# One attention slot on TensorE, in another order

## The chip, the core and the metric

The kernel runs on one core of a Trainium2 chip. The metric is the device time of the whole program in microseconds (us). TensorE (PE) does the matrix products, ScalarE (ACT) the exponentials and most copies out of PSUM, VectorE (DVE) the reductions and the arithmetic on products, GpSimd (POOL) some elementwise work and the indirect DMAs, SyncE (SP) issues the other DMAs. Each engine takes its instructions in the order in which the program gives them; between engines only semaphores order the work.

## The reference

```python
h = _layernorm(x, axis=-1) * (1 + ca) + sa
x = x + ga * _L0_attn_ref(h, ...)      # x is (8, 512, 128), 16 heads of width 8
h = _layernorm(x, axis=-1) * (1 + cb) + sb
x = x + gb * _L0_ffn_ref(h, ...)       # a shared expert, and 2 of 8 routed ones per token

# in _L0_attn_ref, with weights that are binarised (sign times mean magnitude)
att = jnp.einsum('bhtd,bhsd->bhts', q, k) * scale
att = jax.nn.softmax(att, axis=-1)
y = jnp.einsum('bhts,bhsd->bhtd', att, v)
return _binlinear(y, Wp, bp)
```

The attention is dense: for each of the 8 batches and 16 heads there is a 512 x 512 matrix of scores.

## The kernel before, in words

The attention takes most of the time. It runs over the 8 batches (0 to 7), and each batch over 16 **slots** (`SLOTS`). A slot is one group of four heads (`n // 4`) and one quarter of the 512 keys (`n % 4`, 128 keys). Four streams of work run through the slots, each at another distance:

- **scores** (L1446, four in a slot, hh = 0 to 3): a 128 x 512 product of keys and queries of one head, into the score banks `st0` and `st1` in turn. Since there are two banks, each waits on `exp_done` until the exponential of the score two before it is done. Queries and keys are stored as three bf16 parts each, and a row of the stack holds the negated maximum, so that the exponential (L803 on ACT, `pt<-st`) needs no more than a scale.
- **fills** (L1431, two in a slot, each two 128 x 512 products): the scores of a later group, eight slots ahead, for which DVE takes row maxima (`neg_max<-mx`, L1012). The first fill of a slot goes to bank pair `mx0`, the second to `mx1`; each waits on `mx_free` until DVE has reduced the fill before the last. In the first five slots of batch 0 there are three fills. In slots 8 to 15 of batch 7 there are none, and scores 2 and 3 are then written to `mx1`, so that four banks hold scores (`wide`, L345); there a score waits for the exponential of the score four before it.
- the **weighted sum** (L1457, `products`): four 32 x 512 float32 products of one slot's exponentials and values, into `pv`, accumulated over eight slots. It belongs to the slot before and waits for all four exponentials of that slot. The sums that begin an accumulation (those of slots 0 and 8) wait also on `y_evacuated`, the copy of `pv` by ACT (`evacuate_y`, L809).
- **misc work**: one bank, `misc`, for all the small products. `between` (L1524) issues one piece in most slots. In batches 1 to 5 these are: slots 1, 5 and 9 a transpose of maxima (`max_T`, L1364), 2 and 11 a transpose of the weighted sums, 3 a transpose of the normalised sums, 4 the output projection, 7 a transpose of a layer norm, 8 and 14 the projections to queries and keys for the batch two on, 10 a transpose for the second layer norm, 12 the router logits. Slots 0, 6, 13 and 15 have none there. At the end of slot 0 stands the value projection (L1357), at the end of 12 one more transpose of maxima, at the end of 15 the ranks (L1402).

Every order is written by hand. `body` at L1553 gives PE's; `body` at L864 ACT's: four exponentials of slot n, then copies such as `evacuate_y` (after slots 0 and 8), the copy of the value projection (L794, after slot 0) and of the query projection (L788, after slot 8); `body` at L1120 DVE's: the reduction of the first fill, then the work on misc results and layer norms, then the reduction of the second fill. The two buffers `pt` of exponentials alternate by slot.

After the attention come the shared expert (L1590, L1600) and the routed experts (L1646, L1655).

Of the kernel before, what the change touches and what calls it, by code (L numbers as in the profile page):

```python
# [18 lines left out]
SLOTS = G * TT  # L19
# [28 lines left out]
def adaln_block(nc: bass.Bass, x, Wq, bq, Wk, bk, Wv, bv, Wp, bp, sh_gate, sh_up, sh_down,  # L48
                gate_w, up_w, down_w, router_w, routing_bias, c, wmod, out):
    ctx = ExitStack()  # L50
    with ctx:
# [306 lines left out]
        def fill_of(f):  # L358

            b, g = f // (2 * HG * G), f // (2 * HG) % G  # L360
            return Batch(b), g, f // 2 % HG, f % 2
# [958 lines left out]
        def _(pe):  # L1320
# [27 lines left out]
            def project(i, done):  # L1348

                free(done)  # L1350
                pe.matmul(misc[:], wT[:, i, :], hT[:], start=True, stop=True).then_inc(misc_full, 1)  # L1351
# [172 lines left out]
            def between(b, n, first, last):  # L1524
# [25 lines left out]
                if n == 14 and b.const < B - 2:  # L1550
                    project(1, use(b, "k"))

            def body(b, first, last):  # L1553
                for n in range(SLOTS):
                    g, j = n // TT, n % TT
                    fills = fills_at(b, n)
                    if j == 0:
                        pe.wait_ge(m_row_loaded[g % 2], ROW_DMAS * (2 * b.n + g // 2 + 1))
                        if b.const == 0 and g < DIRECT:
                            pe.wait_ge(stack_loaded[0][g], STACK_DMAS)  # L1560
                    scores(b, n, 0)
                    scores(b, n, 1)
                    for f in fills[0]:
                        max_scores(*fill_of(f))
                    between(b, n, first, last)
                    scores(b, n, 2)
                    for f in fills[1][:1]:
                        max_scores(*fill_of(f))
                    scores(b, n, 3)
                    for f in fills[1][1:]:  # L1570
                        max_scores(*fill_of(f))

                    if n > 0:
                        products(b, n - 1)
                    elif not first:
                        products(b.plus(-1), SLOTS - 1)
                    if n == 0 and not last:
                        project_v(use(b, "v"))
                    if n == 12 and not last:
                        max_T(b.plus(1), 0, use(b, "m0"))  # L1580
                    if n == 15 and not first:
                        ranks(b.plus(-1), use(b, "rank"))

            batches(body)
            def shared_up(b, j):

# [128 lines left out]
```

## Time and profile before

| what | us |
|---|---|
| median of 3 runs | 664.68 |
| lowest and highest run | 662.48 to 667.34 |
| the profiled execution, first to last instruction | 683.7 |
| mean granted TensorE clock of it | 0.971 of full speed |

The profiled execution gives no time beside its span. That span is 19.0 us longer than the median of the runs, so the profile is read for its differences and waits, and a difference is carried over to the median as it is. Times in its rows count from the first instruction. A row of the timeline shows a start, a duration, an engine, a line, an operation and a count; rows of like operations are merged. An idle time in brackets is that of the engine before the row, with what ended it. PE durations overlap, since matrix products are pipelined: what a product costs is read from the distance between two starts.

### The profile page before, as it was taken

To read this page: it belongs to the slowest core of one execution; us is meant where nothing else is said; L and a number is where in the kernel's file an instruction comes from. 1 tells how busy PE (TensorE), PEld (TensorE's weight loads), DVE (VectorE), ACT (ScalarE), POOL (GpSimd) and SP (SyncE) were. 2 spreads that over 40 slices of the span, in tenths; PEclk is the share of its full clock that TensorE was granted. 3 is DMA by queue.
4 is the path that set the end of the run, shared out by engine and by line. 5 is a ranking of instruction groups with operands and counts; after the bars stand their busy time and mean duration, and the time that the engine had idled before them with its cause. 6 is when DMAs were issued, how large, how long until landed. Compare 5 with 4: busy or idle time off the path is not lost.

```text
span 683.7 us, 11593 instructions
## 1 busy us (share of the span) xinstructions
PE 624.5 (91%) x3693; PEld 298.9 (44%) x3693; DVE 516.7 (76%) x1104; ACT 411.0 (60%) x846; POOL 264.0 (39%) x309
## 2 busy tenths in 40 slices
PE   4988999999999999999999999999998898888935
PEld 2332333233333333433333333232465888888931
DVE  5659888889988989888898888983368655555617
ACT  2145777777777687777777777778542445444520
POOL 4221022324352461452434233134434366566540
PEclk9669999999999999999999999999999999999987
DMA  3533132222321233223222231115102222222228
GB/s 101 146 56 97 52 101 76 66 82 72 94 86 62 75 97 95 79 78 105 72 70 75 70 98 52 39 40 173 53 0 70 64 74 78 69 78 79 70 68 320
DMA packets 50064, 56.92 MB, mean 83 GB/s; under 512 B 10281, under 2 KB 39243, under 8 KB 50004
## 3 DMA queue, kind: packets, MB, share of 16 engines
q1 hardware_dynamic: 42648, 43.11, 22.4%
q0 software_dynamic: 4320, 8.47, 3.6%
q10 hardware_dynamic: 3036, 4.61, 2.1%
q8 instruction: 30, 0.49, 0.3%
q14 instruction: 30, 0.25, 0.1%
HBM read 38.36 MB, written 17.92 MB: 82 GB/s over the span
## 4 chain that ended last, share of the span: by engine, by line
PE 68%; DVE 13%; ACT 6%; DMA 4%; issue 4%; SPq 2%; POOL 1%; another core or an unknown queue 0%; ACTq 0%; POOLq 0%; DVEq 0%
PE pv L1457 15%; PE st L1446 14%; PE mx L1431 13%; PE st L1646 9%; DVE neg_max L1012 6%; PE mx L1590 3%; ACT pt L803 2%; PE misc L1324 2%; PE misc L1351 2%; PE pv L1655 2%; PE misc L1655 2%; PE st L1600 1%; PE misc L1357 1%; DMA even_qk<-k_parts 1%; DVE ln L969 1%
## 5 line engine op out<-in xcount | busy, mean ns | idle before, releaser
L803 ACT ACTIVATE pt<-st 128x512 f32<-128x512 f32 x496 | 282.2, 598 | 106.0 <-PE st L1446 96.8
L1012 DVE TENSOR_REDUCE neg_max<-mx 128x2 f32<-128x1024 f32 x248 | 294.4, 1215 | 50.5 <-PE mx L1431 47.3
L1457 PE MATMUL pv<-pt,vs 128*32 128x512 f32 x1024 | 136.4, 605 | 0.3 <-ACT pt L803 0.3
L690 POOL DMA_INDIRECT routed<-rec,row_u x64 | 64.4, 1007 | 142.1 <-PE pv L1457 115.2
L750 POOL DMA_INDIRECT results<-qs,home_u x71 | 77.4, 1091 | 60.5 <-ACT qs L932 42.1
L1446 PE MATMUL st<-even_qk 74*128 74x512 bf16 x256 | 88.9, 388 | 4.1 <-DMA even_qk<-m_rows 2.2
L1446 PE MATMUL st<-qs,ks 74*128 74x512 bf16 x240 | 81.5, 383 | 1.8 <-ACT pt L803 1.1
L1431 PE MATMUL mx<-even_qk 72*128 72x512 bf16 x240 | 74.5, 392 | 6.0 <-DVE neg_max L1012 3.4
L1431 PE MATMUL mx<-ks,qs 72*128 72x512 bf16 x256 | 76.5, 380 | 2.8 <-DVE neg_max L1012 2.5
L1258 DVE TENSOR_TENSOR vs<-vs,st 128x256 f32<-128x256 f32 x71 | 29.7, 418 | 42.6 <-ACT vs L927 31.4
L1646 PE MATMUL st<-vs,pt 128*128 128x128 f32 x376 | 52.0, 282 | 10.3 <-DVE vs L1258 7.4
L398 POOL TENSOR_TENSOR qk_r<-qk_f,qk_parts 128x512 f32<-128x512 f32 x15 | 17.4, 1163 | 108.6 <-DVE qk_parts L390 108.4
L927 ACT ACTIVATE vs<-st 128x256 f32<-128x256 f32 x71 | 27.4, 386 | 45.7 <-PE st L1646 35.1
L1446 PEld LDWEIGHTS st<-even_qk 74*128 74x128 bf16 x256 | 20.7, 98 | 73.2 <-ACT pt L803 51.6
L1646 PEld LDWEIGHTS st<-vs,pt 128*128 128x128 f32 x376 | 46.8, 196 | 12.8 <-ACT vs L922 9.1
L1446 PEld LDWEIGHTS st<-qs,ks 74*128 74x128 bf16 x240 | 18.9, 98 | 67.5 <-ACT pt L803 51.6
L1457 PEld LDWEIGHTS pv<-pt,vs 128*32 128x32 f32 x1024 | 20.1, 108 | 52.9 <-issue 38.1
L1431 PEld LDWEIGHTS mx<-even_qk 72*128 72x128 bf16 x240 | 22.3, 100 | 37.9 <-DVE neg_max L1012 11.6
L1431 PEld LDWEIGHTS mx<-ks,qs 72*128 72x128 bf16 x256 | 23.8, 98 | 31.0 <-DVE neg_max L1012 7.8
L1270 DVE COPY pt<-even_qk 128x768 f32 x47 | 27.6, 588 | 6.2 <-issue 3.1
L1590 PE MATMUL mx<-h2T,shared_w 128*128 128x512 f32 x64 | 29.9, 600 | 1.9 <-issue 1.9
L1646 PE MATMUL st<-vs 128*128 128x128 f32 x192 | 25.9, 278 | 3.7 <-DVE vs L1258 2.5
(199 smaller groups left out, 792.7 us busy)
## 6 DMA issues: line engine op xcount, KB each, us to landing
ks<-routed SPq DMA_DIRECT2D x71, 65.0 KB
even_qk<-q_parts SPq DMA_DIRECT2D x48, 96.0 KB
qs<-q_parts SPq DMA_DIRECT2D x48, 96.0 KB
ks<-k_parts SPq DMA_DIRECT2D x48, 96.0 KB
even_qk<-k_parts SPq DMA_DIRECT2D x42, 96.0 KB
q_parts<-qk_parts SPq DMA_DIRECT2D x21, 128.0 KB
k_parts<-qk_parts SPq DMA_DIRECT2D x7, 384.0 KB, 2.3
x_in<-L_attn_x SPq DMA_DIRECT2D x8, 256.0 KB
```

Source lines behind the costliest of these rows:

```text
L690: pool.indirect_dma_start(out=routed_dram, out_offset=bass.IndirectOffsetOnAxis(ap=row_u[:, k, t:t + 1], axis=0), in_=rec[b.par][:, k, t, ...
L750: pool.indirect_dma_start(out=result_dram, out_offset=bass.IndirectOffsetOnAxis(ap=home_u[:, slot:slot + 1], axis=0), in_=y_u[slot], in_of ...
L803: act.activation(pt[n % 2][:, hh, :], score_bank(b, n, hh), ACT.Exp, scale=SCALE).then_inc(exp_done, 1)
L927: act.activation(silu_u[slot % 2], st_bank[slot % 2][:, 0:I], ACT.Silu).then_inc(silu_ready, 1)
L1012: dve.tensor_reduce(neg_max[g % 2][:, hh, 2 * half:2 * half + 2], mx_bank[half][:], AX_X, ALU.max, negate=True).then_inc(mx_free, 1)
L1258: dve.tensor_tensor(act_u[slot % ARING], silu_u[slot % 2], st_bank[slot % 2][:, I:2 * I], ALU.mult).then_inc(act_ready, 1)
L1270: dve.tensor_copy(w_unit[u % WRING], weights.rearrange("p e i -> p (e i)")[:, bass.ds(first, 3 * I)]).then_inc(w_ready, 1)
L1431: last = pe.matmul(mx_bank[half][:, t, :], qs[b.par][0:PROD, h, q0:q0 + P], ks[b.par][0:PROD, h, :], start=True, stop=True)
L1446: pe.matmul(score_bank(b, n, hh), ks[b.par][0:STACK, h, j * P:(j + 1) * P], qs[b.par][0:STACK, h, :], start=True, stop=True).then_inc(st_f ...
L1457: last = pe.matmul(pv_bank[32 * hh:32 * (hh + 1), :], vs[b.par][:, j, HG * g + hh, :], pt[n % 2][:, hh, :], start=(n % Y_SLOTS == 0), stop ...
L1590: last = pe.matmul(mx_bank[j][:, which, :], shared_w[:, IC * which + j, :], h2T[:, T * b:T * (b + 1)], start=True, stop=True)
L1646: last = pe.matmul(st_bank[slot % 2][:, m * P:(m + 1) * P], w_unit[u % WRING][:, m * P:(m + 1) * P], xuT[slot % 2], start=True, stop=True)
```

## The change

In each slot the four scores, two fills, the misc work and the weighted sum of the slot before are put in another order. Nothing is added or taken away, and the instructions of ACT, DVE and SP stay as they are.

```diff
+            def weigh(b, n, first):
+                if n > 0:
+                    products(b, n - 1)
+                elif not first:
+                    products(b.plus(-1), SLOTS - 1)
...
                     scores(b, n, 0)
-                    scores(b, n, 1)
                     for f in fills[0]:
                         max_scores(*fill_of(f))
+                    scores(b, n, 1)
+                    weigh(b, n, first)
+                    scores(b, n, 2)
                     between(b, n, first, last)
-                    scores(b, n, 2)
                     for f in fills[1][:1]:
                         max_scores(*fill_of(f))
                     scores(b, n, 3)
                     for f in fills[1][1:]:
                         max_scores(*fill_of(f))
-
-                    if n > 0:
-                        products(b, n - 1)
-                    elif not first:
-                        products(b.plus(-1), SLOTS - 1)
                     if n == 0 and not last:
                         project_v(use(b, "v"))
```

How the PE instructions then stand, at three places. The first is slot 3 of batch 1, a slot with misc work (the transpose `misc<-ident,y_tok`); `st` are the score banks, `mx` the fills, `pv` the weighted sum. Before:

```order
L1446 MATMUL st0<-qs1,ks1 128x512 [waits exp_done]
L1446 MATMUL st1<-qs1,ks1 128x512 [waits exp_done]
L1431 MATMUL mx0<-ks1,qs1 128x512 [waits mx_free]
L1431 MATMUL mx0<-ks1,qs1 128x512
L1324 MATMUL misc<-ident,y_tok 128x128 [waits misc_free]
L1324 MATMUL misc<-ident,y_tok 128x128 x3
L1446 MATMUL st0<-qs1,ks1 128x512 [waits exp_done]
L1431 MATMUL mx1<-ks1,qs1 128x512 [waits mx_free]
L1431 MATMUL mx1<-ks1,qs1 128x512
L1446 MATMUL st1<-qs1,ks1 128x512 [waits exp_done]
L1457 MATMUL pv<-pt0,vs1 32x512 [waits exp_done]
L1457 MATMUL pv<-pt0,vs1 32x512 x3
```

and after:

```order
L1446 MATMUL st0<-qs1,ks1 128x512 [waits exp_done]
L1431 MATMUL mx0<-ks1,qs1 128x512 [waits mx_free]
L1431 MATMUL mx0<-ks1,qs1 128x512
L1446 MATMUL st1<-qs1,ks1 128x512 [waits exp_done]
L1457 MATMUL pv<-pt0,vs1 32x512 [waits exp_done]
L1457 MATMUL pv<-pt0,vs1 32x512 x3
L1446 MATMUL st0<-qs1,ks1 128x512 [waits exp_done]
L1324 MATMUL misc<-ident,y_tok 128x128 [waits misc_free]
L1324 MATMUL misc<-ident,y_tok 128x128 x3
L1431 MATMUL mx1<-ks1,qs1 128x512 [waits mx_free]
L1431 MATMUL mx1<-ks1,qs1 128x512
L1446 MATMUL st1<-qs1,ks1 128x512 [waits exp_done]
```

The weighted sum stood between score 3 and the next slot's score 0; it now stands between scores 1 and 2, and the misc work stands behind score 2.

The second place is slot 9 of batch 1, where the new accumulation of the weighted sum begins (its first product waits on `y_evacuated`). Before:

```order
L1446 MATMUL st0<-qs1,ks1 128x512 [waits exp_done]
L1446 MATMUL st1<-qs1,ks1 128x512 [waits exp_done]
L1431 MATMUL mx0<-even_qk 128x512 [waits mx_free]
L1431 MATMUL mx0<-even_qk 128x512
L1364 MATMUL misc<-ident,neg_max1 16x128 [waits mx_free,misc_free]
L1446 MATMUL st0<-qs1,ks1 128x512 [waits exp_done]
L1431 MATMUL mx1<-even_qk 128x512 [waits mx_free]
L1431 MATMUL mx1<-even_qk 128x512
L1446 MATMUL st1<-qs1,ks1 128x512 [waits exp_done]
L1457 MATMUL pv<-pt0,vs1 32x512 [waits y_evacuated,exp_done]
```

and after:

```order
L1446 MATMUL st0<-qs1,ks1 128x512 [waits exp_done]
L1431 MATMUL mx0<-even_qk 128x512 [waits mx_free]
L1431 MATMUL mx0<-even_qk 128x512
L1446 MATMUL st1<-qs1,ks1 128x512 [waits exp_done]
L1457 MATMUL pv<-pt0,vs1 32x512 [waits y_evacuated,exp_done]
L1457 MATMUL pv<-pt0,vs1 32x512 x3
L1446 MATMUL st0<-qs1,ks1 128x512 [waits exp_done]
L1364 MATMUL misc<-ident,neg_max1 16x128 [waits mx_free,misc_free]
```

Of the slot's work, two scores, a fill and the transpose of maxima stood ahead of this waiting product and now stand behind it.

The third place is slot 14 of batch 7, without fills and with four score banks (`mx1` holds scores here). Before, to the first score of slot 15:

```order
L1446 MATMUL st0<-qs1,ks1 128x512 [waits exp_done]
L1446 MATMUL st1<-qs1,ks1 128x512 [waits exp_done]
L1446 MATMUL mx1<-qs1,ks1 128x512 [waits exp_done] x2
L1457 MATMUL pv<-pt1,vs1 32x512 [waits exp_done]
L1457 MATMUL pv<-pt1,vs1 32x512 x3
```

and after:

```order
L1446 MATMUL st0<-qs1,ks1 128x512 [waits exp_done]
L1446 MATMUL st1<-qs1,ks1 128x512 [waits exp_done]
L1457 MATMUL pv<-pt1,vs1 32x512 [waits exp_done]
L1457 MATMUL pv<-pt1,vs1 32x512 x3
L1446 MATMUL mx1<-qs1,ks1 128x512 [waits exp_done] x2
```

The weighted sum, which waits for the last exponential of the slot before, now stands ahead of scores 2 and 3.

## Rows read from the trace of the kernel before

**Rows 1.** The page: the chain that ended last, by engine.

```profile
PE 68%; DVE 13%; ACT 6%; DMA 4%; issue 4%; SPq 2%; POOL 1%; another core or an unknown queue 0%; ACTq 0%; POOLq 0%; DVEq 0%
```

**Rows 2.** Windows: one batch: length, busy PE, PEld, DVE, ACT, POOL, clock, DMA.

```profile
109.90:165.60 55.70, 54.52 (x314) 19.39 (x313) 49.50 (x101) 41.34 (x76) 15.88 (x19) 1.00 0.24 72
```

**Rows 3.** Timeline, PE: slot 3 of batch 1, with misc work.

```profile
114.28 0.60 PE L1446 MATMUL st<-qs,ks 74*128 74x512 bf16 x2
114.72 0.60 PE L1431 MATMUL mx<-ks,qs 72*128 72x512 bf16 x2
115.16 0.60 PE L1324 MATMUL misc<-ident,y_tok 128*128 128x128 f32 x4
115.59 0.38 PE L1446 MATMUL st<-qs,ks 74*128 74x512 bf16 x1
...
116.56 1.06 PE L1457 MATMUL pv<-pt,vs 128*32 128x512 f32 x8
117.56 0.39 PE L1446 MATMUL st<-qs,ks 74*128 74x512 bf16 x1
```

**Rows 4.** Timeline, PE: slot 13 of batch 1, without misc work.

```profile
148.90 0.60 PE L1446 MATMUL st<-qs,ks 74*128 74x512 bf16 x2
...
149.97 0.39 PE L1446 MATMUL st<-qs,ks 74*128 74x512 bf16 x1
...
151.94 0.60 PE L1446 MATMUL st<-qs,ks 74*128 74x512 bf16 x2
```

**Rows 5.** Timeline: score 3 of slot 14, batch 1, and its exponential.

```profile
154.51 0.38 PE L1446 MATMUL st<-qs,ks 74*128 74x512 bf16 x1
...
154.93 0.60 ACT L803 ACTIVATE pt<-st 128x512 f32<-128x512 f32 x1 [0.24 <-PE st L1446]
```

**Rows 6.** Timeline: scores 3 of slots 8 and 9, batch 1, and ACT between them.

```profile
134.00 0.38 PE L1446 MATMUL st<-qs,ks 74*128 74x512 bf16 x1
...
135.49 0.60 ACT L809 ACTIVATE y_strips<-pv 128x512 f32<-128x512 f32 x1
135.96 1.10 ACT L803 ACTIVATE pt<-st 128x512 f32<-128x512 f32 x2
...
137.29 0.38 PE L1446 MATMUL st<-qs,ks 74*128 74x512 bf16 x1
```

**Rows 7.** Timeline: DVE in slots 4 to 6 of batch 1, and the fill that waits for it.

```profile
119.77 0.68 DVE L1039 TENSOR_TENSOR x<-misc,x_ep 128x512 f32<-128x512 f32 x1
...
121.55 2.32 DVE L1012 TENSOR_REDUCE neg_max<-mx 128x2 f32<-128x1024 f32 x2
...
125.33 3.47 DVE L1012 TENSOR_REDUCE neg_max<-mx 128x2 f32<-128x1024 f32 x3
126.59 0.60 PE L1431 MATMUL mx<-ks,qs 72*128 72x512 bf16 x2 [0.56 <-DVE neg_max L1012]
```

**Rows 8.** Timeline: weighted sums of slots 4, 7, 12 and 15, batch 1.

```profile
120.29 1.06 PE L1457 MATMUL pv<-pt,vs 128*32 128x512 f32 x8
...
130.62 1.06 PE L1457 MATMUL pv<-pt,vs 128*32 128x512 f32 x8
...
147.79 1.06 PE L1457 MATMUL pv<-pt,vs 128*32 128x512 f32 x8
...
158.08 1.06 PE L1457 MATMUL pv<-pt,vs 128*32 128x512 f32 x8
```

**Rows 9.** Timeline: slots 0 and 1 of batch 2, about the value projection.

```profile
161.25 1.07 PE L1457 MATMUL pv<-pt,vs 128*32 128x512 f32 x8
...
164.66 0.39 PE L1446 MATMUL st<-even_qk 74*128 74x512 bf16 x1 [0.19 <-ACT pt L803]
...
165.63 1.06 PE L1457 MATMUL pv<-pt,vs 128*32 128x512 f32 x8
```

**Rows 10.** Timeline: ACT in slots 14 and 15 of batch 7, without fills.

```profile
478.30 1.09 ACT L803 ACTIVATE pt<-st 128x512 f32<-128x512 f32 x2
...
480.26 1.08 ACT L803 ACTIVATE pt<-st 128x512 f32<-128x512 f32 x2
```

## The prediction, made before the changed kernel ran

> **What bounds the kernel now.** I read the chain of waits first: 68% of it is PE and 13% DVE [rows 1], so the order of PE's own work decides. Then one whole batch by windows: in 55.70 us DVE is busy 49.50 and ACT 41.34 [rows 2]; the window runs from the weighted sum of slot 1 in one batch to that in the next. Busy PE (54.52) says little, because its durations overlap, so I take the distances between starts in the timeline. In a slot with misc work [rows 3] they are: two scores 0.44 (0.22 each), first fill 0.44, misc 0.43, then 0.97 from score 2 to the weighted sum (score 2 and the second fill as before 0.22 + 0.44, so score 3 takes 0.31), weighted sum 1.00: 3.28 us, and PE waits for nobody. Without misc work the same pieces are 2.85, but the slot takes 3.04 [rows 4]: score 2 starts 1.07 after score 0, where the pieces between them are 0.88. It waits for the first exponential, which frees its bank. That is one round through ACT: 0.42 from the start of a score to that of its exponential, 0.60 of exponential [rows 5], 0.05 until PE goes on. So the old slot is the larger of 3.04 and 2.85 + misc: the misc work lies inside the round from score 0 to score 2, and where there is some, the round costs nothing. The other round, from score 3 to the next slot's score 1, is covered by the weighted sum.
>
> **What the change does to a slot.** Work and distances are the same, 2.85 + misc. Two rounds matter. Score 2 to the next score 0 now has the misc work, the second fill (0.44), score 3 (0.22) and score 2's own 0.22 in it, 0.88 + misc: as tight as before and as well covered by misc work. The new one is score 3 to the next score 1: behind score 3 stand score 0 and the first fill, 0.22 + 0.22 + 0.44 = 0.88, and score 1 must not start before 1.07 or 1.08. The weighted sum that covered this round is now queued behind the waiting score, and so are score 2, the misc work and the second fill. From score 3 to score 3 a slot is 1.08 + 0.31 + 1.00 + 0.22 + misc + 0.44 = 3.05 + misc, always. Without misc work that is the old 3.04; with it each slot loses 0.20.
>
> **A steady batch (1 to 5), by slots.** I carried this recurrence through 16 slots, with DVE's reductions at 1.15 each when they queue (3.47 for three, the last ending 1.2 after its start [rows 7]).
> - Slots 2, 3, 4, 8, 10, 11, 12: 0.20 each, less 0.1 since slot 2 had a small wait already: **+1.3**.
> - Slots 5 to 7: DVE comes late out of slot 4, where the copy, statistics and a reduction chain start at 119.77 and the next reductions at 121.55, 1.8 later, and behind them a fill waits 0.56 for it [rows 7]. In the new order the misc result comes behind the weighted sum, so DVE idles about 1.2 between its first reduction and the work on that result; in slot 4 it had just enough slack before. From the weighted sum of slot 4 to that of slot 7 it takes 10.33 [rows 8]; I get 10.65: **+0.3**.
> - Slot 9: the weighted sum of slot 8 begins an accumulation and waits for ACT's copy of the old one. Behind score 3 of slot 8 ACT has the exponential, the query copy and that copy, which starts 1.49 after the score and takes 0.60 [rows 6]: 2.14 until PE may start, where the new order would come at 1.08 + 0.31 = 1.39. Before, a whole slot of work lay between. From score 3 to score 3 the slot is 3.9 against 3.29 [rows 6]: **+0.6**.
> - Slots 13 to 15: before they took 10.29 [rows 8], where the pieces alone would be 3 x 2.85 + 0.87 for the projection = 9.4, the rest being waits; the new order spaces the two fills 1.7 and 1.1 apart instead of 0.9 and 2.0, and feeds DVE more evenly: 10.0, **-0.3**.
> - Slots 0 and 1: before, the weighted sum, the value projection and then ACT's copy of its result stood in a row, and slot 1 took 165.63 - 161.25 = 4.38, with score 2 waiting for ACT [rows 9]. Now the weighted sum is out earlier and ACT has copied `pv` before the value projection ends; the copies are covered by score 0, a fill, score 1 and a weighted sum. I get 6.9 for both slots. Before it was 165.63 - 158.08 = 7.55 [rows 8, 9]: **-0.7**.
> Sum +1.2 a batch, 5 batches: **+6.0**.
>
> **The other batches.** Batch 0: the same small loss in six slots with misc work and in slot 9, less the gain at its end: +0.9. Its first five slots have three fills (3.45 of DVE each) and are bound by DVE; both orders let it idle about 0.3 a slot, so I put nothing there, and 1.5 either way in the range. Batch 6 has no projections and loses +0.3. Batch 7, slots 2 to 7: +0.5. Its slots 8 to 15 have no fills and four score banks, and there ACT never stops: a slot takes 480.26 - 478.30 = 1.96, four exponentials 0.49 apart [rows 10]. There a score need only wait for one four before it, but the new order puts the weighted sum, which waits for the last exponential of the slot before, ahead of scores 2 and 3. From the start of that exponential: 0.60 + 0.05, then the weighted sum 1.00, then score 2 at 1.65 and its exponential at 2.08, while the two exponentials queued last only to 1.58. ACT runs dry for half a microsecond in each slot: 2.57 instead of 1.96 in slots 13 to 15 (+1.8), and less in slots 9 to 12, which misc work and the copies already lengthened (+0.8); slot 8 gains 0.4, because the weighted sum now fills the wait for the last reductions. +2.2.
> Sum: 6.0 + 0.9 + 0.3 + 0.5 + 2.2 = 9.9, say **+10**. No DMA or POOL instruction moves; the routed scatter waits by slot only, and shifts with them. The profiled span is 683.7, 19.0 above the median of the runs, and has no other time beside it; I carry the difference over: 693.7 there, and 664.7 + 10 = **674.7 us** as the time of a run.
>
> **A price the trace of before does not show** is the wait of score 1 behind a fill. Its bounds: nothing, if the 1.07 of [rows 4] were ACT's pace for two exponentials in a row (the second starts only 0.49 behind the first, and score 3 has none of its slot behind it), and 0.44, if a product that waits also loses the overlap of its weight load with the one ahead. I take 0.20: the exponential of a lone score 3 starts after the same 0.42 [rows 5]. Over some 50 slots with misc work that is -10 to +12 on the sum, of which the far ends are unlikely.
>
> **A page's rule against the row.** By the chain and the distances above PE fills the slot. The Trainium skill, Perfetto Trace Analysis, section Identifying the Most-Contended Engine, says that matmul busy time is no good measure and that LDWEIGHTS busy time and the FLOPs used should be taken instead, and that the engine with the highest occupancy is the one to improve. By that rule DVE would be the bound, PEld being far below it, and the change would be judged by how it feeds DVE: the sum of rival B below, -6, where the rows give +10. The trace agrees that busy PE is no measure, yet the distances of [rows 3] leave PE no gap.
>
> **Rivals.**
> - **A: the new wait does not show.** The 0.20 is zero, by the lower bound. Then the steady batch is -0.3 + 0.6 + 0.3 - 0.7 = about 0, and what is left is batch 7's end: +2.5, 667 us. For it: the margin is only 0.2 of a 1.08 round. Against: exactly this round shows in every slot without misc work. Chance 0.18.
> - **B: DVE is what counts** (faster). DVE is busy 89% of a batch [rows 2]; fills now come evenly spaced, and its waits vanish: the 0.56 in slot 6 [rows 7], about 0.6 of the 0.9 in slots 13 to 15, and the 0.7 of slots 0 and 1, 1.9 a batch for the 6 with projections, 11.4 in all, less 2.2 at the end and less the 0.6 of slot 9 in each: 9.2 - 3.6 = 5.6, or 659 us. It decides if score 1 does not wait. Against: misc results now reach DVE later than its first reduction ends, so that it idles more, not less. Chance 0.08.
> - **C: DVE's new idle time adds up.** Where DVE works on misc results (slots 1, 2, 4, 5, 9, 11, 12) it waits up to 1 us for each; with 55.70 - 49.50 = 6.2 us of slack a batch [rows 2], three slots that cannot absorb it cost 1.5 to 2 a batch more than I have: 686 us. Chance 0.12.
> - That the change does not do what it says can be put aside: the PE rows moved as described, and no other engine's did.
> My forecast has the rest, 0.62.
>
> **The numbers.** 674.7, with its own range of 670 to 680. The range reaches to A below and into C above: 666 to 684. About 1% (6.6 us) can be told from no change. Slower by more than that (above 671.3): 0.55 of the forecast's 0.62 and all of C, 0.68. Within 1%: A, the low edge of the forecast, and a part of B, 0.25. Faster: 0.07.
>
> **What will show it.** In a steady slot with misc work: 3.5 us instead of 3.28, score 1 starting 1.08 after the last score 3, with ACT as what it waited for. In slot 9 a weighted sum that waits about 0.7 for `evacuate_y`. Slot 1 near 3.8 after the value projection, with no wait on score 2. In the last slots of batch 7 a period of 2.6 with ACT idle before each third exponential. It is wrong if a slot with misc work stays at 3.28, or if the fills wait for DVE in more than slots 6 and 7.

## The result: 2.7% slower

| | before | changed |
|---|---|---|
| median, us (runs) | 664.66 (4) | 682.37 (4) |
| lowest to highest | 662.48 to 667.34 | 681.32 to 684.09 |
| ratio of the times | | 1.0274, interval 1.0242 to 1.0306 |
| profiled execution: its time, its span | span 683.7 | 681.32, span 679.6 |

The changed kernel takes 17.7 us longer. 674.7 was forecast, in a range of 666 to 684: the direction and the mechanism hold, the loss was put at 10 and is 17.7.

The two spans, 683.7 before and 679.6 after, say the opposite of the two medians. The same code of the routed experts took 124.3 us in the first profile of the kernel before, and 103.0 in that of the changed one. A second profile of the kernel before (`before_again`, below) has a span of 657.8 and 103.3 for the experts, with the same attention to 0.1 us. So the 21 us were a disturbance of that one execution, outside the attention; its cause is open. The rows ahead of the prediction stand, but the 19.0 us that the prediction carried over to a profiled span of 693.7 do not: that span is 679.6.

Since the start of the attention also moves by some us from one execution to the next, the traces are compared by the **length of the attention**, from the start of the first weighted sum to the start of the last. The time is a median where the table says how many runs it is from, else that of the one profiled run. The kernel before took 665.7 to 666.4 beside the experiments, and the ratios given below are to those runs.

| kernel | length, us | time, us (runs) |
|---|---|---|
| before, two profiles | 429.9, 429.9 | 664.7 (4) |
| changed | 446.5 | 682.4 (4) |
| `swap_only` | 426.4 | 662.0 (10) |
| `sum_at_end` | 441.8 | 678.8 (4) |
| `sum_only` | 511.2 | 744.0 |
| `slot9_late` | 451.1 | 683.3 |
| `wide_late` | 448.4 | 686.3 |
| `misc_early` | 462.0 | 693.9 |
| `y_copy_first` | 443.1 | 677.5 |
| `half_exp_before`, `half_exp_after` | 427.6, 427.3 | 663.0, 660.3 |
| `slot0_early` | 428.3 | 663.6 (10) |
| `combined` | 425.4 | 661.5 (12) |

In the changed kernel the very first weighted sum comes ahead of score 2, the later fills and score 3 of its slot, where it stood behind them. Those 1.3 us (0.22 + 0.44 + 0.44 + 0.22) lie inside the length now and lay outside before, so the true excess is about 15 of the 16.7: 15.4 by this count, and 14.7 if the work is counted from score 3 of that slot, where the old order had a wait for DVE. The same holds for the other kernels with the weighted sum in the middle of the slot.

### The profile after

The chain of waits of the changed kernel, shares by engine, to set beside [rows 1]. PE's share is larger, 73% against 68%, but that says nothing of the order: the second profile of the kernel before, with the same attention, has 56%, and `swap_only`, the faster kernel, 72%. The bound has to be read from the slots, below.

```profile
PE 73%; DVE 13%; ACT 5%; DMA 4%; issue 2%; SPq 1%; POOL 1%; ACTq 0%; DVEq 0%; POOLq 0%
```

One batch by windows, from the weighted sum issued in slot 1 of batch 1 to that in slot 1 of batch 2, as [rows 2]: 1.7 us longer, with DVE and ACT no busier.

```profile
111.60:169.00 57.40, 55.48 (x317) 19.83 (x317) 49.34 (x101) 40.72 (x76) 15.81 (x19) 1.00 0.23 65
```

Slot 3 of batch 2 in the timeline, PE, PEld (its weight loads) and ACT, the slot of [rows 3] in the new order:

```profile
174.24 0.59 PE L1446 MATMUL st<-even_qk 74*128 74x512 bf16 x2
174.65 1.68 ACT L803 ACTIVATE pt<-st 128x512 f32<-128x512 f32 x3 [0.49 <-PE st L1446]
174.67 0.59 PE L1431 MATMUL mx<-even_qk 72*128 72x512 bf16 x2
175.30 0.10 PEld L1446 LDWEIGHTS st<-even_qk 74*128 74x128 bf16 x1 [0.53 <-ACT pt L803]
175.31 0.39 PE L1446 MATMUL st<-even_qk 74*128 74x512 bf16 x1
175.63 1.06 PE L1457 MATMUL pv<-pt,vs 128*32 128x512 f32 x8
176.62 0.39 PE L1446 MATMUL st<-even_qk 74*128 74x512 bf16 x1
176.85 0.60 PE L1324 MATMUL misc<-ident,y_tok 128*128 128x128 f32 x4
...
177.29 0.60 PE L1431 MATMUL mx<-even_qk 72*128 72x512 bf16 x2
177.72 0.60 PE L1446 MATMUL st<-even_qk 74*128 74x512 bf16 x2
```

The first row is score 3 of slot 2 and score 0 of slot 3, merged. Score 1 starts at 175.31: 1.07 after score 3, and 0.64 after the fill before it, where 0.44 is the bare distance. PE's row shows no idle time, because the duration of the fill covers the gap; the distance shows the wait, and the row of the weight load just before names its end, ACT's exponential. From score 3 to score 3 the slot takes 177.72 - 174.24 = 3.48 instead of 3.28.

Slot 9 of the same batch, score 1 and the weighted sum behind it, to set beside [rows 6]. The weighted sum waits 0.77 for ACT's copy of `pv`:

```profile
197.29 0.39 PE L1446 MATMUL st<-even_qk 74*128 74x512 bf16 x1
198.44 1.07 PE L1457 MATMUL pv<-pt,vs 128*32 128x512 f32 x8 [0.77 <-ACT y_strips L809]
```

ACT between them, from the exponential of score 3 to that of the next score 0, each 0.5 to 0.6 behind the other:

```profile
196.63 0.60 ACT L803 ACTIVATE pt<-st 128x512 f32<-128x512 f32 x1 [0.91 <-PE st L1446]
197.13 0.68 ACT L788 ACTIVATE qk_f<-misc,bias_qkv 128x512 f32<-128x512 f32 x1
197.70 0.60 ACT L809 ACTIVATE y_strips<-pv 128x512 f32<-128x512 f32 x1
198.18 1.10 ACT L803 ACTIVATE pt<-st 128x512 f32<-128x512 f32 x2
```

Slots 13 to 15 of batch 7, without fills, where [rows 10] showed an ACT that never stops. Timeline, PE and ACT:

```profile
493.29 1.07 PE L1457 MATMUL pv<-pt,vs 128*32 128x512 f32 x8 [0.53 <-ACT pt L803]
494.29 0.60 PE L1446 MATMUL mx<-qs,ks 74*128 74x512 bf16 x2
494.72 1.09 ACT L803 ACTIVATE pt<-mx 128x512 f32<-128x512 f32 x2 [0.50 <-PE mx L1446]
494.74 0.59 PE L1446 MATMUL st<-qs,ks 74*128 74x512 bf16 x2
495.69 1.09 ACT L803 ACTIVATE pt<-st 128x512 f32<-128x512 f32 x2
495.86 1.06 PE L1457 MATMUL pv<-pt,vs 128*32 128x512 f32 x8 [0.53 <-ACT pt L803]
```

Weighted sums stand 2.57 apart instead of 1.96. Each waits for the last exponential, scores 2 and 3 come a full weighted sum later, and ACT is idle for 0.50 until their products are there. Both engines wait, one after the other.

### The profile page after: what moved, and what is told of

It is laid out like the page before. It is cut to its first block, busy times and chain, and to the rows that moved or that the text cites. A ratio compares the mean times of both kernels' runs of the same rounds, so it can differ in the third digit from the quotient of the medians.

```text
span 679.6 us, 11593 instructions
## 1 busy us (share of the span) xinstructions
PE 626.9 (92%) x3693; PEld 299.7 (44%) x3693; DVE 516.6 (76%) x1104; ACT 412.3 (61%) x846; POOL 265.0 (39%) x309
## 4 chain that ended last, share of the span: by engine, by line
PE 73%; DVE 13%; ACT 5%; DMA 4%; issue 2%; SPq 1%; POOL 1%; ACTq 0%; DVEq 0%; POOLq 0%
PE pv L1457 16%; PE st L1446 15%; PE mx L1431 13%; PE st L1649 9%; DVE neg_max L1012 6%; PE mx L1593 3%; ACT pt L803 3%; PE pv L1658 2%; PE misc L1324 2%; PE misc L1658 2%; PE misc L1351 2%; PE st L1603 1%; DMA even_qk<-k_parts 1%; PE mx L1638 1%; PE misc L1381 1%
## 5 line engine op out<-in xcount | busy, mean ns | idle before, releaser
L1012 DVE TENSOR_REDUCE neg_max<-mx 128x2 f32<-128x1024 f32 x248 | 291.1, 1211 | 35.2 <-PE mx L1431 34.9
L1446 PE MATMUL st<-even_qk 74*128 74x512 bf16 x256 | 93.2, 389 | 3.2 <-DMA even_qk<-m_rows 1.5
L1446 PE MATMUL st<-qs,ks 74*128 74x512 bf16 x240 | 84.8, 383 | 2.0 <-ACT pt L803 0.2
L1446 PEld LDWEIGHTS st<-even_qk 74*128 74x128 bf16 x256 | 24.8, 97 | 103.4 <-ACT pt L803 86.0
L1446 PEld LDWEIGHTS st<-qs,ks 74*128 74x128 bf16 x240 | 23.0, 96 | 91.6 <-ACT pt L803 77.7
L1649 PE MATMUL st<-vs,pt 128*128 128x128 f32 x376 | 49.7, 275 | 0.0
L1593 PE MATMUL mx<-h2T,shared_w 128*128 128x512 f32 x64 | 31.3, 628 | 1.9 <-DVE pt L1162 1.9
L901 ACT ACTIVATE pt<-mx 128x512 f32<-128x512 f32 x16 | 9.6, 598 | 29.4 <-PE mx L1593 29.3
```

The source lines that it names most:

```text
L1012: dve.tensor_reduce(neg_max[g % 2][:, hh, 2 * half:2 * half + 2], mx_bank[half][:], AX_X, ALU.max, negate=True).then_inc(mx_free, 1)
L1446: pe.matmul(score_bank(b, n, hh), ks[b.par][0:STACK, h, j * P:(j + 1) * P], qs[b.par][0:STACK, h, :], start=True, stop=True).then_inc(st_f ...
L1593: last = pe.matmul(mx_bank[j][:, which, :], shared_w[:, IC * which + j, :], h2T[:, T * b:T * (b + 1)], start=True, stop=True)
L1649: last = pe.matmul(st_bank[slot % 2][:, m * P:(m + 1) * P], w_unit[u % WRING][:, m * P:(m + 1) * P], xuT[slot % 2], start=True, stop=True)
```

## The experiments

The theory: a score may not start until the exponential two scores before it is done, one **round** of 1.07 to 1.08 us. The old order leaves one round bare (score 0 to 2, 0.88 of work in it), and misc work lies in it. The new order leaves bare the round from score 3 to the next score 1, and no misc work lies in that. Rivals: the place of the weighted sum or of the fill as such; DVE starved by misc results that come late.

### A second profile of the kernel before

> The kernel before, unchanged, for a second profile. In the first one the routed experts took 124.3 us from their first product (532.55) to their last weighted product (656.85), in the changed kernel 103.0 (549.83 to 652.81), with code that is the same. If that was a disturbance of the one profiled execution, this profile has a span near 663, the experts take about 103, and the attention ends near 482.4 as in the first. If the changed kernel really speeds the experts, they take 124 again.

Measured: 659.58 us, span 657.8; the attention starts at 47.9 instead of 52.5 and has the same length, slot by slot within 0.01 to 0.05; the experts take 103.3. It was a disturbance. The earlier start goes with TensorE's granted clock: 1.00 from 40 to 50 us here, 0.50 in the changed kernel's profile. (It was 0.66 in the first profile of the kernel before.) Over all the profiles here the first weighted sum starts between 47.9 and 54.3, whatever the order: that part of a run is some us of chance.

### One part of the change: only the weighted sum moves

```diff
                     between(b, n, first, last)
+                    if n > 0:
+                        products(b, n - 1)
+                    elif not first:
+                        products(b.plus(-1), SLOTS - 1)
                     scores(b, n, 2)
...
-                    if n > 0:
-                        products(b, n - 1)
-                    elif not first:
-                        products(b.plus(-1), SLOTS - 1)
```

> The kernel before with one part of the change: the weighted sum of the slot before goes ahead of score 2 and all else stays (score 0, score 1, first fill, misc, weighted sum, score 2, second fill, score 3). Theory (the round through ACT from score 3 to the next score 1 must be covered): behind score 3 only score 0 stands, 0.22 + 0.22 before score 1 can start where 1.08 is needed, so a slot is 1.08 + 0.22 + 0.44 + misc + about 0.1 + 1.00 + 0.22 + 0.44 = 3.5 + misc against 3.04 and 2.85 + misc before: about 0.4 to 0.6 a slot, and 45 to 55 us in all, near 715. Rival (what costs in the change is DVE's idle time behind late misc results): the misc work stays early here, so no more than 5 us, near 668.

Measured: 744.0 us, length 511.2. Slot 3 of batch 1, PE's timeline:

```profile
124.81 0.81 PE L1446 MATMUL st<-qs,ks 74*128 74x512 bf16 x2
125.88 0.39 PE L1446 MATMUL st<-qs,ks 74*128 74x512 bf16 x1 [0.26 <-ACT pt L803]
126.11 0.60 PE L1431 MATMUL mx<-ks,qs 72*128 72x512 bf16 x2
126.55 0.60 PE L1324 MATMUL misc<-ident,y_tok 128*128 128x128 f32 x4
127.08 1.07 PE L1457 MATMUL pv<-pt,vs 128*32 128x512 f32 x8
128.07 0.39 PE L1446 MATMUL st<-qs,ks 74*128 74x512 bf16 x1
128.30 0.60 PE L1431 MATMUL mx<-ks,qs 72*128 72x512 bf16 x2
128.74 0.88 PE L1446 MATMUL st<-qs,ks 74*128 74x512 bf16 x2
```

The first row is score 3 (124.81) and the next score 0, and score 1 follows at 125.88, 1.07 later. The slot takes 128.74 - 124.81 = 3.93, against 3.48 in slots without misc work: the 3.5 + misc of the theory, to 0.05. The rival's 668 is out: here the misc work is as early as before. That accounts for about 50 us (an estimate: a steady batch is 62.8 when its slots at full clock are added up, against 55.8 before; five of them are 35, and the other three batches some 5 or 6 each). The other 25 to 30 go with something that the expectation did not have. In some of slots 12 to 14 of the steady batches, and in a few slots of batches 0 and 7, the fills' products stand 0.43 apart instead of 0.22, and windows of the same trace show the clock with them (columns as in [rows 2], with GB/s of DMA last):

```profile
226.00:230.00 4.00, 3.84 (x21) 1.75 (x22) 1.84 (x3) 1.28 (x4) 0.00 (x0) 0.76 0.02 4
230.00:234.00 4.00, 3.95 (x12) 0.93 (x14) 2.35 (x4) 2.34 (x5) 0.00 (x0) 0.50 0.01 3
...
242.00:250.00 8.00, 7.50 (x45) 2.34 (x42) 6.16 (x10) 5.42 (x10) 2.92 (x3) 1.00 0.00 0
```

The granted clock is 0.50, the lower of its two levels (1.2 GHz), for about 14 us; most slots before it are 0.6 to 0.8 us longer than in the kernel before, by waiting alone, since the work is the same. That the waiting brings the clock down is not shown by a run of its own. In the changed kernel it stays at 1.00 from 110 to 400 us.

### The other part: only score 1 and the first fill change places

```diff
                     scores(b, n, 0)
-                    scores(b, n, 1)
                     for f in fills[0]:
                         max_scores(*fill_of(f))
+                    scores(b, n, 1)
                     between(b, n, first, last)
```

> The kernel before with the other small part: only score 1 and the first fill change places. Theory: the weighted sum still covers the round from score 3 to the next score 1, and score 0 to score 2 is 0.88 + misc as before; steady slots stay at 3.04 and 3.28, and the time within 3 us of 664.7. Rival (a score that follows a fill comes too late for ACT): 0.2 in each of some 110 slots, near 685.

Measured: ratio 0.995, interval 0.991 to 0.999; length 426.4, slots 3.28 with misc work and 3.05 without. The swap alone costs nothing and takes 3.5 off the length: slots 2, 5 and 14, which waited for DVE or ACT in the old order, are 0.10, 0.17 and 0.18 shorter (3.38, 3.27 and 3.88 before). DVE gets its first fill 0.22 earlier. I had put this at nothing.

### The change with the weighted sum back at the end

```diff
                     scores(b, n, 1)
-                    weigh(b, n, first)
                     scores(b, n, 2)
                     between(b, n, first, last)
...
                     for f in fills[1][1:]:
                         max_scores(*fill_of(f))
+                    weigh(b, n, first)
```

> The changed kernel with the weighted sum put back at the end of the slot: score 0, first fill, score 1, score 2, misc, second fill, score 3, weighted sum. Theory: now the round from score 0 to score 2 is bare (0.88 against 1.08) because the misc work stands behind it, so a slot with misc work is again 3.05 + misc, 0.2 longer than before; but slot 9 does not wait for ACT's copy and the last eight slots of batch 7 are as before. The gain in slots 0 and 1 is gone too. About 1.6 a steady batch and 11 us in all, near 676. Rival (the place of the weighted sum alone is what costs): near 665.

Measured: ratio 1.020, interval 1.014 to 1.027; length 441.8. Its slots are 3.49 with misc work and 3.05 without, the last ones of batch 7 1.96. Slot 3 of batch 1, PE's timeline:

```profile
115.27 0.39 PE L1446 MATMUL st<-qs,ks 74*128 74x512 bf16 x1
115.50 0.60 PE L1431 MATMUL mx<-ks,qs 72*128 72x512 bf16 x2
115.93 0.81 PE L1446 MATMUL st<-qs,ks 74*128 74x512 bf16 x2
116.58 0.60 PE L1324 MATMUL misc<-ident,y_tok 128*128 128x128 f32 x4
```

The third row is scores 1 and 2, merged. The misc work follows score 2 by 0.23, so score 2 starts at 116.35, 1.08 after score 0 (115.27). The weighted sum is back in its old place and the 0.2 a slot is still lost, now to the round from score 0 to score 2, because the misc work stands behind score 2. So what costs 0.2 a slot is that the misc work lies outside the bare round, not where the weighted sum stands.

### The changed kernel with shorter exponentials

```diff
-                    act.activation(pt[n % 2][:, hh, :], score_bank(b, n, hh), ACT.Exp, ...)
+                    w = T if b.const == 0 and n < 2 else T // 2
+                    act.activation(pt[n % 2][:, hh, 0:w], score_bank(b, n, hh)[:, 0:w], ACT.Exp, ...)
```

The same edit was made in both kernels.

> The changed kernel with exponentials of half the columns (256 of 512; the other half of pt keeps old values, so the output is not the reference's), except in the first two slots. The round through ACT falls from 1.08 to about 0.85, below the 0.88 of work that stands in it. Theory: slots with misc work go to 2.85 + misc, 3.28, the others to 2.85 where DVE lets them, and the attention's length to about 430, though PE does the same work. Rival (PE work or its order is dearer in itself): slots with misc work stay near 3.49.

Measured: length 427.3 instead of 446.5. Slot 3 of batch 1 (lines are one further down in this kernel):

```profile
115.18 1.06 PE L1458 MATMUL pv<-pt,vs 128*32 128x512 f32 x8
...
117.28 0.60 PE L1447 MATMUL st<-qs,ks 74*128 74x512 bf16 x2
117.71 0.59 PE L1432 MATMUL mx<-ks,qs 72*128 72x512 bf16 x2
118.14 0.38 PE L1447 MATMUL st<-qs,ks 74*128 74x512 bf16 x1
118.45 1.07 PE L1458 MATMUL pv<-pt,vs 128*32 128x512 f32 x8
```

Score 1 (118.14) now follows the fill by 0.43, and the slot takes 3.27. PE's work and order are those of the changed kernel; only ACT's time is less.

> The kernel before with exponentials of half the columns (the other half of pt keeps old values, so the output is not the reference's), to set beside the changed kernel with the same halving, whose attention takes 427.3 us from the first to the last weighted sum (446.5 with whole exponentials). Theory (the longer time is the uncovered round through ACT): slots without misc work go from 3.04 to about 2.85, those with it stay at 3.28, and the length is 422 to 425, so that the 16.7 us between the two orders shrink to 3 to 5, what is left being slot 9 and the last slots of batch 7. Rival (the order is dearer whatever ACT takes): near 411, 16 less than 427.3.

Measured: length 427.6. With short rounds the two orders are as good as equal (427.3 and 427.6), where they were 16.7 apart. That they come out quite equal is luck: slots 15 and 0 at the end of batch 6 took 5.20 and 3.83 here, 2.6 more than elsewhere, with a granted clock of 0.89 from 420 to 450 us. Without that the length would be about 425 and the difference 2.3, near the 3 to 5 that the theory left; the 422 to 425 that it gave for this kernel is missed by the same 2.6. The steady batches are 55.3 in this kernel and 55.2 in the changed one with the same halving. DVE is busy 49 us in both; that it now sets their pace is argued, not shown.

### Slot 9

```diff
                     scores(b, n, 1)
-                    weigh(b, n, first)
+                    if not (n == Y_SLOTS + 1):
+                        weigh(b, n, first)
                     scores(b, n, 2)
...
                     for f in fills[1][1:]:
                         max_scores(*fill_of(f))
+                    if n == Y_SLOTS + 1:
+                        weigh(b, n, first)
```

> The changed kernel, but in slot 9 of each batch the weighted sum that waits for ACT's copy of pv goes back to the end of the slot. The length from the first to the last weighted sum of the attention is 446.5 in the changed kernel and 429.9 in the one before; in its slots 8 to 9 that distance is 4.74. Theory (a wait of about 0.8 for the copy, per batch): 8 x 0.7 = 5.5 less, near 441. Rival (the wait is only moved to another instruction, since ACT is late anyway): within 1.5 of 446.5.

Measured: not better but worse. The two distances from the weighted sum issued in slot 8 to that in slot 10 are 6.22 + 1.97 = 8.19, where the changed kernel has 4.74 + 3.16 = 7.90. What waits instead is score 2, and longer:

```profile
201.20 0.39 PE L1446 MATMUL st<-even_qk 74*128 74x512 bf16 x1 [1.16 <-ACT pt L803]
```

The rival holds: ACT's two copies delay the next exponential too, so with the weighted sum gone from the middle nothing covers that wait. (Another 3.2 us of this run's length, around slot 10 of batch 1, go with some 7 us at a granted clock of 0.50 there.)

```diff
+                    if n == Y_SLOTS:
+                        evacuate_y(b, 0)
                     if n == 8 and b.const < B - 2:
                         evacuate_qk(b.plus(2), 0, use(b, "q"))
...
-                    if n == Y_SLOTS:
-                        evacuate_y(b, 0)
```

> The changed kernel, with ACT's copy of pv ahead of its copy of the query projection after slot 8 (both still follow the slot's exponentials). Moving the waiting weighted sum to the end of slot 9 only moved the wait to score 2, since both copies delay the next exponential. Theory: here the copy that the weighted sum waits for ends 0.6 earlier, while the next exponential comes when it did; the distance between the weighted sums of slots 8 and 9 falls from 4.74 to about 4.2 in batches 0 to 5, and the attention's length from 446.5 to about 443. Rival (score 2 waits anyway): 4.74 stays within 0.1.

Measured: 4.74 falls to 4.16 or 4.17 in batches 0 to 5, and the length to 443.1:

```profile
195.95 1.06 PE L1457 MATMUL pv<-pt,vs 128*32 128x512 f32 x8 [0.19 <-ACT y_strips L809]
```

So the wait of slot 9 was for the copy of `pv`, and most of it goes by a change in ACT's order, where moving PE's product did not help.

### The last slots of batch 7

```diff
-                    weigh(b, n, first)
+                    if not (wide(b, n)):
+                        weigh(b, n, first)
...
                     for f in fills[1][1:]:
                         max_scores(*fill_of(f))
+                    if wide(b, n):
+                        weigh(b, n, first)
```

> The changed kernel, but in slots 8 to 15 of batch 7 (no fills, four score banks) the weighted sum goes back to the end of the slot. Theory: ACT does not run dry there, the period of the last slots falls from 2.56 to 1.96, and the length from the first to the last weighted sum falls from 446.5 by 3.5 to 5, to about 442.3; nothing else changes. Rival (PE or the misc work bounds these slots): under 1 less.

Measured: batch 7, from its first weighted sum to its last, takes 502.41 - 460.3 = 42.1 instead of 498.42 - 452.7 = 45.7 (before: 40.6). The period is 1.96 again, by ACT:

```profile
498.33 1.09 ACT L803 ACTIVATE pt<-st 128x512 f32<-128x512 f32 x2
...
500.29 1.09 ACT L803 ACTIVATE pt<-st 128x512 f32<-128x512 f32 x2
```

3.6 of the change's loss is this. The run's whole length (448.4) and time (686.3) are no measure of it: its batch 0 took 65.1 where the changed kernel's took 59.7, with the granted clock at 0.50 until 68.5 us.

### Misc work ahead of score 1

```diff
                     for f in fills[0]:
                         max_scores(*fill_of(f))
+                    between(b, n, first, last)
                     scores(b, n, 1)
                     weigh(b, n, first)
                     scores(b, n, 2)
-                    between(b, n, first, last)
```

> The changed kernel with the misc work between the first fill and score 1. Theory: now the misc work covers the round from score 3 to the next score 1 and leaves bare the one from score 2 to the next score 0 (0.22 + 0.44 + 0.22 = 0.88 against 1.08), so a slot with misc work stays at 3.05 + misc, 3.49; only what waited for DVE (slots 5 to 7) gains, some 0.3 a batch, and the attention's length is 443 to 446.5. Rival (late misc results starve DVE, and that is the loss): slots with misc work fall to 3.28 and the length to about 434.

Measured: 462.0, longer than either expectation. Slots 2, 3, 7 and 10 take 3.48 or 3.49: the bare round has moved and costs the same, and the rival's 3.28 is out. Slot 6 falls from 3.79 to 3.05: DVE gets its misc work earlier, and the longer slot 4 gives it time too; which of the two counts is not shown. What neither foresaw: four slots a batch (1, 4, 8 and 11) are 0.4 to 0.9 longer than in the changed kernel, since misc work so early in a slot waits for an ACT copy, and holds all of PE. In slot 11:

```profile
209.09 0.66 PE L1324 MATMUL misc<-ident,y_strips 128*128 128x128 f32 x4 [0.81 <-ACT h2T L818]
```

### Two versions that should beat both

```diff
                     between(b, n, first, last)
+                    early = n == 0 and not first and not last
+                    if early:
+                        products(b.plus(-1), SLOTS - 1)
                     scores(b, n, 2)
...
-                    elif not first:
+                    elif not first and not early:
                         products(b.plus(-1), SLOTS - 1)
```

> The kernel before with one part of the change in slot 0 of batches 1 to 6 alone: there the weighted sum of the slot before goes ahead of score 2, where the value projection at the end of the slot covers the round that it leaves. Theory: slots 0 and 1 fall from 7.55 to about 6.9, 0.65 x 6 = 4 us in the attention's length (429.9 to 426), and the time to about 661. Rival (another wait takes its place, DVE's in slots 1 to 3): under 1.

Measured: length 428.3, ratio 0.998 (0.996 to 1.000). Slots 0 and 1 fall from 7.55 to 2.09 + 5.24 = 7.33, and slot 2 from 3.38 to 3.29: 0.3 a batch, 1.6 in all, where the theory had 4 and the rival under 1. The gain that the prediction gave to these slots needs the rest of the new order as well.

`combined` is this, with the swap of `swap_only` in most slots, and in slots 1, 9 and 13 (6 and 7 too in batches 6 and 7) the old order with one product of the second fill ahead of score 2:

```diff
+                    split = b.const > 0 and (n in (1, 9, 13) or b.const >= B - 2 and n in (6, 7))
                     scores(b, n, 0)
+                    if split:
+                        scores(b, n, 1)
                     for f in fills[0]:
                         max_scores(*fill_of(f))
+                    if not split:
+                        scores(b, n, 1)
                     between(b, n, first, last)
...
+                    for f in fills[1][:split]:
+                        max_scores(*fill_of(f), ts=(0,))
                     scores(b, n, 2)
                     for f in fills[1][:1]:
-                        max_scores(*fill_of(f))
+                        max_scores(*fill_of(f), ts=(1,) if split else (0, 1))
```

> Put together what the runs point to: the kernel before with the first fill ahead of score 1 (which took 3.4 off the attention's length by itself), the weighted sum early in slot 0 of batches 1 to 6 (about 4), and in slots 1, 9 and 13 (and 6 and 7 of the last two batches) score 1 ahead of the fill as before and the first product of the second fill ahead of score 2, to fill the 0.2 that score 2 waits where misc work is short (0.2 in two or three slots a batch, less what DVE takes back: 2). Attention 420 to 423 against 429.9, and the time 656 to 659 against 664.7. Rival (DVE, 49.5 busy of 55.7 a batch, takes the gain back): 424 or more.

Measured: ratio 0.996, interval 0.993 to 0.999; length 425.4, 1.0 better than the swap alone, and 4.5 better than before. The expected 420 to 423, and 656 to 659 for the time, did not come; the rival holds. Slot 13 falls from 3.15 to 2.98 and slot 14 behind it rises from 3.70 (in `swap_only`) to 4.05, because its second fill now waits for DVE's reduction:

```profile
208.26 0.61 PE L1431 MATMUL mx<-ks,qs 72*128 72x512 bf16 x2 [0.18 <-DVE neg_max L1012]
```

Slots 0 and 1 gain 0.37 and slot 2 gives 0.17 back. The batch takes 55.2 (55.3 in `swap_only`), with DVE busy 48.75 in 55.00 of it:

```profile
105.00:160.00 55.00, 54.13 (x317) 19.40 (x313) 48.75 (x101) 41.84 (x75) 14.33 (x19) 1.00 0.26 72
```

The best here is 0.4% or 0.5% faster than the kernel before, by `combined` or `swap_only`, which can't be told apart in time.

## Why the prediction was right, and 7.7 short

| term | forecast | measured |
|---|---|---|
| slots 2, 3, 4, 8, 10, 11, 12 of a steady batch | +1.3 | +1.5 |
| slots 5 to 7 | +0.3 | 10.65 - 10.33 = +0.3 |
| slot 9 | +0.6 | 3.99 - 3.29 = +0.7 |
| slots 13 to 15 | -0.3 | 10.00 - 10.29 = -0.3 |
| slots 0 and 1 | -0.7 | 6.97 - 7.55 = -0.6 |
| a steady batch | +1.2 | +1.6 |
| five of them | +6.0 | +8.2 |
| batch 0 | +0.9 | +1.5 |
| batch 6 | +0.3 | +1.1 |
| batch 7 | +2.7 | +4.0 |
| the first slots, and outside the attention | 0 | about 2.9 |

The steps stand in the order of the forecast. Each slot is taken from score 3 to score 3, and each batch from slot 2 to slot 1 of the next. At the end of batch 7 one weighted sum, 1.0, is counted on the side of the new order, since it stands ahead of the first score 3 there and stood behind it before. The sum is 14.8 for the attention.

**The round.** Score 1 starts 1.07 after score 3, a slot with misc work takes 3.48, and with halved exponentials it takes 3.27. Slot 1 takes 3.84, and the last slots of batch 7 2.57, as the signs of the prediction had it. That the wait comes out at its likeliest value and at neither bound (0 or 0.44) is shown by the row of 175.31. Rival A is out.

**Mis-sized: the steady batch.** The seven slots gave 1.5 and not 1.3: slot 11 took 3.64 and not 3.49, because behind slot 10 ACT makes two copies (L817, L818) before the next exponential. I had costed ACT's copies only in slots 0 and 8. Slot 9, and slots 0 and 1, gave 0.1 more each, and the rest is rounding: +1.6 instead of +1.2, times five batches, is 2.2 of the 7.7 that are missing.

**Mis-sized: the end of batch 7.** I had +2.2 for slots 8 to 15 and `wide_late` shows 3.6. The period of 2.57 came as worked out. The -0.4 of slot 8 came too (2.61 instead of 3.00). Mis-sized are slots 9 to 12: together 12.19 instead of 10.47, +1.7 where I had +0.8, most of it in slot 9 (3.26 instead of 2.08), whose weighted sum waits for ACT's copy:

```profile
479.40 1.06 PE L1457 MATMUL pv<-pt,vs 128*32 128x512 f32 x8 [1.11 <-ACT y_strips L809]
```

Left out was the very last weighted sum: before, it came 482.38 - 480.80 = 1.58 after the one before it, and now 498.42 - 495.86 = 2.56, since scores 2 and 3 of the last slot, and so their exponentials, now come behind the one before it.

**Mis-sized: batches 0 and 6**, together 1.4 short. In batch 0, slots 2 to 5, which have three fills or follow them and were put at nothing, take 18.15 instead of 17.55: that 0.6 is the whole of its miss, at a granted clock of 1.00. In batch 6, slots 9 to 12 take 14.40 instead of 13.43, and slots 13 and 14 give back 0.7. The prediction did not split its +0.3 by slots, and no run took this batch apart, so its cause stays open.

**Outside the attention**, where I had nothing: from the last weighted sum to the first product of the experts it takes 51.4 instead of 50.1, with the granted clock at 0.91 from 530 to 550 us. In seven of the fourteen profiles, this one among them, the clock is at 0.50 for 3.4 us in that stretch, and all seven take 1.3 to 1.6 us longer there than the other seven, which are at 1.00 throughout. `half_exp_before`, `slot0_early` and `combined`, all versions of the old order, are among the longer ones, so it is not tied to the change. Of the rest, 0.6 is the choice of where the attention starts, and the last 1 us or so is within the spread of the runs.

**Slot 9** of the steady batches: the price was right, and so was what it waits for (`y_copy_first`), but taking the weighted sum out of the way doesn't give it back (`slot9_late`).

**Rival B** (DVE is what counts) was wrong for this change, whose DVE is as busy as before and whose batches are longer. It fits the next one: once the rounds are short or covered, batches stop at 55.2 or 55.3 in four kernels (`swap_only`, `combined` and both with halved exponentials), with DVE busy 49 of it. No run shortened DVE's work to test that. The rule of the Trainium skill quoted in the prediction (Perfetto Trace Analysis, Identifying the Most-Contended Engine) points at what seems to limit further gains here, not at what a new order costs: DVE was as busy in one kernel as in the other, and the order of PE's work made the difference. **Rival C** did not come: in slots 5 to 7 DVE's idle time cost 0.3, as forecast.

Two slips in the prediction itself: the chance of slower by more than 1% is 0.55 + 0.12 = 0.67 by its own terms, not 0.68; and its first step, that PE's 68% of the chain shows PE's order to decide, rests on a share that was 56% in the second profile of the same kernel. The distances of [rows 3, 4] carry the argument without it.

## What to carry to other kernels

When two buffers alternate between two engines, each buffer has a round trip of its own, and an order of work is as good as its least covered round. Add up the work inside every round, not only that of the slot: here one round of 1.08 us had 0.88 us in it in either order, and the 0.2 us a slot came from where the optional work lay. Once a wait is covered, look for the engine that is next before counting on its gain: here slot 2 gave back half of what slots 0 and 1 gained, and in slot 14 a wait for DVE took twice what slot 13 gained.

## What the runs showed of the hardware

- In `sum_only` waits of about 0.6 us in most slots came with drops of the granted clock from 1.00 to 0.50 within the steady batches, the one shown for about 14 us, although no single wait on PE in that trace is listed above 0.4 us from 120 to 450 us. With waits of 0.2 us a slot (the changed kernel, `sum_at_end`, `y_copy_first`) it stayed at 1.00 from 110 to 400 us. The loss was 79 us, of which about 50 (an estimate, above) are the waits themselves. Such drops are not confined to this order: `half_exp_before` and `slot9_late` had one of 7 us each in their attention.
- A wait of 0.2 us between overlapping products leaves no idle time in PE's rows; it shows as a longer distance between starts (0.64 instead of 0.44) and before the weight load (0.53 idle, ended by ACT).
- One profiled execution of the kernel before had 21 us more in code that a second execution ran in 103.3: a span alone can point the wrong way. The shares of the chain moved as well: PE had 68% in the one and 56% in the other.
